# Table stage of a token-embedding, attention and mixture-of-experts kernel: 128 partitions in place of 125, the angle product on TensorE, rounding on ScalarE, clamps and scalings on GpSimd

## What is computed

```python
# token table: rows with is_num become sines of number times frequency
freqs = arange(1, 129)
scaled = num_value / 1000
sin_table = sin(scaled[:, None] * freqs[None, :])        # 12500 x 128
table = where(is_num[:, None], sin_table, weight)
h = table[x]                                             # x: 128 x 128 ids
# attention with mixed heads (8 heads of 64, 128 sequences of 128 tokens)
h = h + attn(layernorm(h), Wq, Wkv, scale, mix_pre, mix_post, Wout, bout)
# a shared expert and two banks of 8 experts, top 1, capacity 1280 rows
h = h + ffn(layernorm(h), ...)
```

## Time and profile before

| | us |
|---|---|
| median of three executions | 1666.71 |
| lowest and highest | 1663.58, 1667.42 |
| span of the profiled execution, first to last instruction | 1659.7 |
| the median above that span | 7.0 |
| busy in the span: PE, PEld, DVE, ACT, POOL | 1495.3, 1377.3, 1119.0, 1149.3, 1129.5 |
| first instruction of the stage after `setup` | 113.40 |

### The profile page before, as it was taken

One profiled execution on the slowest core, in us unless ns is written; L12 is line 12 of the kernel. 1 busy time (PEld: TensorE's weight loads), 2 busy tenths in 40 slices (PEclk: granted clock), 3 DMA queues, 4 the chain that ended last, 5 costly groups with the idle time before them and its releaser, 6 DMA issues. The chain is left out here.

```text
span 1659.7 us, 37390 instructions
## 1 busy us (share of the span) xinstructions
PE 1495.3 (90%) x11183; PEld 1377.3 (83%) x11183; DVE 1119.0 (67%) x2864; ACT 1149.3 (69%) x3478; POOL 1129.5 (68%) x1105
## 2 busy tenths in 40 slices
PE   4306999999999999999999999987999988879999
PEld 2105999999989989989989999877999988879999
DVE  8957778878878777877878887752332444456555
ACT  3416988888888888888888888853555544445554
POOL 8835556787878878878878786656700767766665
PEclk8659999999999999999999999998999999989999
DMA  3332220000000000000000000002443555533333
GB/s 132 133 111 94 105 90 15 28 27 27 18 19 19 17 18 16 14 15 14 15 15 15 14 15 7 3 5 62 110 114 106 135 137 141 130 77 87 86 87 84
DMA packets 112855, 97.75 MB, mean 59 GB/s; under 512 B 26417, under 2 KB 98285, under 8 KB 112676
## 3 DMA queue, kind: packets, MB, share of 16 engines
q1 hardware_dynamic: 90896, 58.18, 11.4%
q0 software_dynamic: 20480, 31.01, 8.3%
q10 hardware_dynamic: 1300, 6.40, 1.0%
HBM read 53.96 MB, written 52.54 MB: 64 GB/s over the span
## 5 line engine op out<-in xcount | busy, mean ns | idle before, releaser
L774 ACT ACTIVATE expd<-masked,nmax 128x128 f32<-128x128 f32 x1024 | 395.9, 393 | 0.0
L585 POOL TENSOR_TENSOR prob<-expd,rtotal 128x1024 f32<-128x1024 f32 x128 | 243.3, 1901 | 134.1 <-DVE rtotal L852 133.6
L869 DVE COPY_PREDICATED masked<-off_diag,ps_s 128x1024 f32<-128x1024 int32 x128 | 175.2, 1369 | 139.3 <-PE ps_s L672 139.3
L714 PE MATMUL ps_o<-u,probT 128*128 128x128 f32 x2048 | 249.1, 275 | 0.7 <-issue 0.7
L714 PEld LDWEIGHTS ps_o<-u,probT 128*128 128x128 f32 x2048 | 239.0, 191 | 0.9 <-issue 0.9
L1352 POOL DMA_INDIRECT fq_back<-answered_sp,fq_back_i x128 | 122.5, 957 | 137.2 <-DVE fq_back_i L1313 103.0
L774 ACT ACTIVATION_READ_ACCUMULATOR expd<-masked,nmax 128x1 f32 x1024 | 196.9, 192 | 0.0
L783 ACT ACTIVATE u<-ps_ut 128x1024 f32<-128x1024 f32 x128 | 131.4, 1027 | 68.8 <-PE ps_ut L725 68.8
L797 ACT ACTIVATE probT<-ps_ut 128x1024 f32<-128x1024 f32 x128 | 131.6, 1028 | 51.3 <-PE ps_ut L680 44.7
L884 DVE TENSOR_TENSOR w_lo<-ps_w,w_hi 128x512 fp32r<-128x512 f32 x256 | 163.9, 680 | 4.4 <-ACT w_hi L804 4.4
L804 ACT ACTIVATE w_hi<-ps_w 128x512 fp32r<-128x512 f32 x256 | 146.2, 596 | 16.5 <-PE ps_w L702 10.0
(11 more groups left out here) (236 smaller groups left out, 4099.0 us busy)
## 6 DMA issues: line engine op xcount, KB each, us to landing
out<-sh_res SPq DMA_DIRECT2D x56, 128.0 KB, 2.3
h_sb<-in_L_tok_weight SPq DMA_DIRECT2D x10, 625.0 KB
table<-h_sb ACTq DMA_DIRECT2D x10, 625.0 KB
sent_sp<-zeros SPq DMA_DIRECT2D x8, 640.0 KB, 3.0
sent_fq<-zeros SPq DMA_DIRECT2D x8, 640.0 KB, 2.9
rows<-sent_sp SPq DMA_DIRECT2D x40, 128.0 KB, 3.1
answered_sp<-sp_res SPq DMA_DIRECT2D x40, 128.0 KB
rows<-sent_fq SPq DMA_DIRECT2D x40, 128.0 KB, 3.6
```

The lines of the kernel that those rows point to most:

```text
L585: nc.gpsimd.tensor_tensor(prob[k % 2][:, :].rearrange("p (g j) -> p g j", g=H), expd[k % 2][:, :].rearrange("p (g j) -> p g j", g=H), rtot ...
L714: mm = nc.tensor.matmul(ps_o[:, 0:D], probT[k % 2][:, g * N:(g + 1) * N], u[k % 2][:, g * D:(g + 1) * D], start=(g == 0), stop=(g == H - 1))
L774: ins = nc.scalar.activation(expd[(k - 1) % 2][:, g * N:(g + 1) * N], masked[(k - 1) % 2][:, g * N:(g + 1) * N], ACT.Exp, bias=nmax[(k - 1 ...
L869: nc.vector.copy_predicated(masked[k % 2][:, :].rearrange("p (g j) -> p g j", g=H), off_diag[:, :].unsqueeze(1).to_broadcast([P, H, N]), p ...
```

## The change

- The table lies over 128 partitions, 97 rows in each, and the 84 rows that are left over form a 98th column on 84 partitions. Chunks have 8 rows (128 x 1024 values, 512 KB); there are 12 of these and one of 2 rows, 13 in all.
- PE turns the numbers (13 small products into `numT`), and then makes the angles: `numT` (8 numbers by 128 partitions) times `freq`, a block diagonal of 8 x 1024, into PSUM (`ps_a`, two buffers). Two products of 512 columns a chunk, with 8 rows of contraction.
- ACT finds the whole turns in two passes (1024 values from PSUM, then in place in SBUF), with the rounding constant as its bias, and takes the sine in place.
- DVE's two steps now read and write `ps_a`, the second writes `angle` in SBUF. DVE puts the sines of chunk c-2 where it was c-1.
- POOL clamps each chunk, and scales the 8 pieces with one instruction each (`mix`), and fills `masked`.
- `ps_m` holds both matrices in turn, so the fifth product waits for the low part of the first matrix.
- SP loads one chunk ahead of the other inputs, keeps four in flight, and issues all stores itself, after the loads.

The core of the diff:

```diff
-VP = 125
-VR = VOCAB // VP
-VC = 10
+VR = VOCAB // P
+REST = VOCAB - VR * P
+VS = VR + 1
+VC = 8
+CHUNKS = -(-VS // VC)
...
+        ps_a = [pb(f"ps_a{k}", CH) for k in range(2)]
+        ps_m = pb("ps_m", H * D)
+        ps_t = pb("ps_t", 512)
+        ps_c = pb("ps_c", 512)
...
+            def clamp(c):
+                a = angle[c % 3][:, 0:rows_of(c) * D]
+                pool.wait_ge(S["reduced"], c + 1)
+                nc.gpsimd.tensor_scalar(a, a, PI_BELOW, -PI_BELOW, ALU.min, ALU.max).then_inc(S["clamped"], 1)
+
+            def mix(c):
+                nc.gpsimd.tensor_tensor(mixed[:, c, :].rearrange("p (g d) -> p g d", g=H),
+                                        mix_src[:, c, :].unsqueeze(1).to_broadcast([P, H, D]),
+                                        mix_co[:, c, :].unsqueeze(2).to_broadcast([P, H, D]), ALU.mult).then_inc(S["mixed"], 1)
+
+            def prefill(k):
+                link.inc(nc.gpsimd.tensor_copy(masked[k][:, :].rearrange("p (g j) -> p g j", g=H),
+                                               diag[:, :].unsqueeze(2).to_broadcast([P, H, N])))
+
+            for c in range(CHUNKS):
+                clamp(c)
+                if c == 2:
+                    pool.wait_ge(S["coef_out"], 2)
+                    pool.wait_ge(S["wT_out"], 1)
+                if 2 <= c < 2 + 2 * HC:
+                    mix(c - 2)
+                if c == 2 + 2 * HC:
+                    prefill(0)
+                    prefill(1)
...
+            link(nc.gpsimd.memset(zeros[:, :], 0.0))
...
+            sp.dma_start(num_i[:, 0:VR], num_value[0:P * VR].rearrange("(p r) -> p r", p=P)).then_inc(S["num"], 16)
+            sp.dma_start(isn[:, 0:VR], is_num[0:P * VR].rearrange("(p r) -> p r", p=P)).then_inc(S["num"], 16)
+            sp.wait_ge(S["made"], made["pads"])
+            sp.dma_start(num_i[0:REST, VR:VS], num_value[P * VR:VOCAB].rearrange("(p o) -> p o", o=1)).then_inc(S["num"], 16)
+            sp.dma_start(rest_isn[0:REST, 0:1], is_num[P * VR:VOCAB].rearrange("(p o) -> p o", o=1)).then_inc(S["num"], 16)
+            sp.dma_start(h_sb[:, cols(0)], w_main[:, cols(0)]).then_inc(s_row[0], 16)
...
+            for c in range(1, CHUNKS - 1):
+                need(sp, s_row[c % 4], 16 * (c // 4))
+                sp.dma_start(h_sb[:, cols(c)], w_main[:, cols(c)]).then_inc(s_row[c % 4], 16)
+            one = slice((CHUNKS - 1) * CH, VR * D)
+            sp.wait_ge(s_row[(CHUNKS - 1) % 4], 16 * ((CHUNKS - 1) // 4))
+            sp.dma_start(h_sb[:, one], w_main[:, one]).then_inc(s_row[(CHUNKS - 1) % 4], 16)
+            sp.dma_start(h_sb[0:REST, LAST_COL], weight[P * VR:VOCAB, :]).then_inc(s_row[(CHUNKS - 1) % 4], 16)
...
+            for c in range(CHUNKS - 1):
+                sp.wait_ge(S["done"], c + 1)
+                sp.dma_start(t_main[:, cols(c)], h_sb[:, cols(c)]).then_inc(S["put"], 16)
+            sp.wait_ge(S["done"], CHUNKS)
+            sp.dma_start(t_main[:, one], h_sb[:, one]).then_inc(S["put"], 16)
+            sp.dma_start(table[P * VR:VOCAB, :], h_sb[0:REST, LAST_COL]).then_inc(S["put"], 16)
+            sp.wait_ge(S["put"], 16 * (5 + CHUNKS + 1))
...
+            def whole_turns(c):
+                w = rows_of(c) * D
+                act.wait_ge(S["angle"], c + 1)
+                need(act, S["reduced"], c - 1)
+                t = turns[c % 2][:, 0:w]
+                nc.scalar.activation(t, ps_a[c % 2][:, 0:w], ACT.Copy, bias=ROUND, scale=INV_TWO_PI).then_inc(S["whole"], 1)
+                act.wait_ge(S["whole"], 2 * c + 1)
+                nc.scalar.activation(t, t, ACT.Copy, bias=-ROUND).then_inc(S["whole"], 1)
+
+            def sines(c):
+                a = angle[c % 3][:, 0:rows_of(c) * D]
+                act.wait_ge(S["clamped"], c + 1)
+                nc.scalar.activation(a, a, ACT.Sin).then_inc(S["sine"], 1)
+
+            for c in range(CHUNKS + 1):
+                if c < CHUNKS:
+                    whole_turns(c)
                 if c:
+                    sines(c - 1)
+                if 1 <= c <= 3:
+                    act.wait_ge(S["wT"], c)
+                    dst = (mix_src[:, 0:HC, :], wkT[:, :, :], wvT[:, :, :])[c - 1]
+                    nc.scalar.activation(dst.rearrange("p c n -> p (c n)"), ps_t[:, :], ACT.Copy).then_inc(S["wT_out"], 1)
+                if c == 1:
+                    act.wait_ge(S["coefd"], 1)
+                    nc.scalar.activation(mix_co[:, :, :].rearrange("p c h -> p (c h)"), ps_c[:, 0:2 * HC * H], ACT.Copy).then_inc(S["coef_out"], 1)
+                    nc.scalar.activation(diag[:, :], ps_c[:, 128:128 + H], ACT.Copy).then_inc(S["coef_out"], 1)
+                for w in range(2):
+                    if c == (8, CHUNKS)[w]:
+                        act.wait_ge(S["M"], w + 1)
+                        nc.scalar.activation(mats["MN"[w] + "_hi"][:, :], ps_m[:, :], ACT.Copy).then_inc(S["hi"], 1)
...
+            def angles(c):
+                n = rows_of(c)
+                pe.wait_ge(S["made"], made["freq"])
+                pe.wait_ge(S["numT_out"], 1 if c < 2 else 4)
+                need(pe, S["reduced"], c - 1)
+                for at in range(0, n * D, 512):
+                    w = min(512, n * D - at)
+                    ins = nc.tensor.matmul(ps_a[c % 2][:, at:at + w], numT[0:n, c * P:(c + 1) * P], freq[0:n, at:at + w],
+                                           start=True, stop=True)
+                ins.then_inc(S["angle"], 1)
...
+            def product(c):
+                w = c // HC
+                if c == HC:
+                    pe.wait_ge(S["lo"], 1)
+                if c == 0:
+                    pe.wait_ge(S["wT_out"], 2)
+                if c == HC:
+                    pe.wait_ge(S["wT_out"], 3)
+                pe.wait_ge(S["mixed"], c + 1)
+                for half in range(2):
+                    at = slice(half * 512, (half + 1) * 512)
+                    ins = nc.tensor.matmul(ps_m[:, at], (wkT, wvT)[w][:, c % HC, :], mixed[:, c, at],
+                                           start=(c % HC == 0), stop=(c % HC == HC - 1))
+                if c % HC == HC - 1:
+                    ins.then_inc(S["M"], 1)
+
+            for c in range(CHUNKS):
+                angles(c)
+                if c == 1:
+                    turn(0)
+                    coefficients()
+                if c in (2, 3):
+                    turn(c - 1)
+                if 4 <= c < 4 + HC:
+                    product(c - 4)
+                if c >= 9:
+                    product(HC + c - 9)
...
+            def reduce(c):
+                w = rows_of(c) * D
+                a, t, out = ps_a[c % 2][:, 0:w], turns[c % 2][:, 0:w], angle[c % 3][:, 0:w]
+                dve.wait_ge(S["whole"], 2 * c + 2)
+                link(nc.vector.scalar_tensor_tensor(a, t, -TWO_PI_HI, a, ALU.mult, ALU.add))
+                nc.vector.scalar_tensor_tensor(out, t, -TWO_PI_LO, a, ALU.mult, ALU.add).then_inc(S["reduced"], 1)
 
             def put_sines(c):
+                n = rows_of(c)
+                dve.wait_ge(s_row[c % 4], 16 * (c // 4 + 1 + (c == CHUNKS - 1)))
+                dve.wait_ge(S["sine"], c + 1)
+                nc.vector.copy_predicated(h_sb[:, cols(c)].rearrange("p (r d) -> p r d", r=n),
+                                          mask[:, c * VC:c * VC + n].unsqueeze(2).to_broadcast([P, n, D]),
+                                          angle[c % 3][:, 0:n * D].rearrange("p (r d) -> p r d", r=n)).then_inc(S["done"], 1)
...
+                reduce(c)
+                if c >= 2:
+                    put_sines(c - 2)
+                if c == 2:
+                    dve.wait_ge(S["coefd"], 1)
                     link.inc(nc.vector.tensor_copy(ids[:, :], ps_c[:, 256:384]))
+                    dve.wait_ge(S["made"], made["rank_i"])
+                    link.inc(nc.vector.tensor_copy(C.rank[:, :], C.rank_i[:, :]))
+                if c == 9:
+                    low(0)
+            put_sines(CHUNKS - 2)
             put_sines(CHUNKS - 1)
+            low(1)
```

More of the change, by code:

```diff
@@ L266, in setup @@
-        block = s.enter_context(nc.Block())
-        def chunk(c):
-            return slice(c * CH, (c + 1) * CH)
+        ps_a = [pb(f"ps_a{k}", CH) for k in range(2)]
+        ps_m = pb("ps_m", H * D)
+        ps_t = pb("ps_t", 512)
+        ps_c = pb("ps_c", 512)
+        names = ("made", "num", "num_f", "numT", "numT_out", "angle", "whole", "reduced", "clamped", "sine", "done", "put",
+                 "weights", "wT", "wT_out", "coef", "coefd", "coef_out", "mixed", "M", "hi", "lo")
+        S = {n: sem("s_" + n) for n in names}
@@ L375, in _ @@
         @block.tensor
         def _(pe):
-            pe.wait_ge(s_const, 8)
-            pe.wait_ge(s_small, 112)
-            for c in range(HC):
-                nc.tensor.transpose(ps_t[0][:, c * P:(c + 1) * P], wq[:, c * P:(c + 1) * P], ident[:, :])
-                nc.tensor.transpose(ps_t[1][:, c * P:(c + 1) * P], wkv[:, c * P:(c + 1) * P], ident[:, :])
```

(26 more changed lines are left out.)

242 lines of the change are left out of this document (100 added, 142 removed).

## The result

| us | before | changed |
|---|---|---|
| median (lowest to highest) | 1666.99 (1663.58 to 1667.42) | 1642.39 (1639.63 to 1644.99) |
| profiled execution, its own time | 1661.5 | 1641.4 |
| its span | 1659.7 | 1639.6 |
| barrier (SP's first issue of the next stage) | 113.40 | 90.94 |
| barrier to the first masked copy of attention | 25.7 | 28.8 |

The changed kernel takes 0.9862 of the time before [0.9844, 0.9879] (brackets behind a ratio hold its 95% interval), 24.6 us less. An execution's own time stands 1.8 us above its span (1641.4 to 1639.6); 1661.5 is worked out with that. The barrier is the end of the stage, read as SP's first issue behind it.

A forecast was written before the change was run, and what follows sets the result against it. DVE's list and 132 GB/s transfers bound the stage together. Front 29.9, chunks to 60.7, wait to 75.2 and tail put the barrier at 89.7, 23.7 us earlier: span 1636.0 plus 7.0 gives 1643.0, range 1635 to 1658.

The forecast's parts named there:

- Two limits side by side: Stage before: DVE's list to 104.4 and transfers to 112.4; lifting only one leaves the other holding.
- Transfers: Large loads and stores: 128 partitions give 410 GB/s instead of 132, 12.8 MB in 31 us, under DVE's work.
- DVE's new steps: DVE's two steps per chunk: 1.22 us each, not lengthened by POOL because one operand lies in PSUM.
- The slower rival: POOL lengthens DVE's new steps as the old: 6.9 per chunk, 30 us in all, total 1673; 4 in 100.
- Period 4.3: Middle chunks 3 to 8: 8.6 us for two chunks, 4.3 each, six chunks ending at 55.7.
- a ring: Middle chunks: clamp, sine, ACT's passes, DVE's reducing and a 1.28 wait for the copy in sequence, 7.9 for two chunks.
- The front, 29.9 for chunk 2: Stage start: numbers ready at 7.5, first chunk reduced at 19.4, chunk 2 reduced at 29.9 us.
- From chunk 4 on I take it so: PE in the middle chunks: 3.4 us of full-clock work in 4.3 keeps the clock up from chunk 4.
- The rival of the low clock: PE stays at 1.2 GHz since 8-row products don't hold it; 6.9 us a chunk, total 1657; 12 in 100.
- The hole: After chunk 9: fifth product waits for `M_lo`, chunk 10's angles queue behind; 14.5 us, from 60.7 to 75.2.
- The tail: Chunks 11 and 12, last copies, store issues and landing: from 75.2 to the barrier at 89.7.
- From the barrier to the total: After the stage: the barrier's 23.7 us gain passes whole to the span, plus 7.0 from span to median: 1643.0.

The follow-up runs named there:

- 1: The kernel before with each large transfer cut into partitions 0 to 111 and 112 to 124; 1658.10, ratio 0.9964.
- 2: The changed kernel with its large transfers cut into 125 and 3 partitions; 1658.25, ratio 0.9970.
- rows128_step: The changed kernel with angle products padded to 128 rows and DVE's second step reading two SBUF inputs; one execution, barrier at 93.66, no total given.
- 7: The changed kernel with one wait added, so POOL builds the frequencies only after DVE has made the numbers; ratio 0.9879.
- after_again: The changed kernel unedited, run again on another chip; 1790.12, ratio 0.9896 to before on that chip, barrier at 96.13.
- 8: The changed kernel with 50 unused products of 512 columns on PE ahead of its attention list; ratio 0.9868.

## Why the prediction was right, and where not

The time came out within 1 us, 1643.0 and 1642.4, and the mechanism was the one forecast: two limits side by side, both lifted, and a new wait after `M_lo`. That it came so near is luck: the steps behind it were off by up to 3.7 us each, and their errors cancel.

- **Two limits side by side.** Right, and the experiments 1 and 2 show it: 6.2, 3.8, and 22.5 together.
- **Transfers.** Right: the share of 0.31 is gone with the 125 partitions, and came back with them in 2. The Trainium skill, "DMA: Bandwidth & Descriptors", section "Why a DMA increments its semaphore by 16 and not by 1", says that the engines are the largest k up to 16 that divides the slowest dimension of both sides, here the partitions. The rows agree: a share of 0.94 with 112, 0.33 with 125.
- **DVE's new steps**, 1.22 each: right throughout. The slower rival (steps as long as before) needed what rows128_step made, 2.45.
- **Period 4.3**: without low clock it was 3.85. I had added 0.7 of handovers per two chunks and 1.28 for the clamp behind the copy. The clamp does wait, 0.96 (2.00 for 1.04). The Trainium skill, "SBUF — State Buffer", section "Who interferes with whom", states the lock, and the trace agrees on it (2.00 and, in rows128_step, 2.45). But in the changed kernel it costs next to nothing, because 2.00 + 1.89 on POOL are no more than 0.1 above DVE's 3.83. I had priced a ring where two engines' own lists bind.
- **The front, 29.9 for chunk 2**: 32.6. The number steps took 4.65 us (4.53 to 9.18) beside POOL's building of `freq`, and 2.5 without it (7). I had let POOL's work there cost nothing. The 13 pieces took 5.3, not 2.8, since each is two records at 0.21 and I took one. But the first angles were through 2.0 us after their start (14.65 to 16.67), not 3.8: the clock that I had down was up. So the first reduced chunk came at 21.3 for 19.4, and the third angles began at 24.2 for 23.4. The other 2.1 of the 2.7 come behind that: these angles took 3.78, where I had the clock up and 1.7. I had the clock the wrong way round twice.
- **"From chunk 4 on I take it so"**, the clock at full: the step that failed most. Chunks 3 to 8 took 29.5 where 25.8 stood; with 128 rows, 24.8. The rival of the low clock was given 12 in 100; it held for about half the stage (18 to 41 and 52 to 55 us, and the product after the hole), and where it held a chunk with angles and piece takes PE 7.42, not the 6.9 of the prediction. Its argument (few rows don't hold it) was right as far as the runs with 8 and with 128 rows go, and my argument against it (short gaps) was not: PE had no gaps at all from 18 to 40 us. The Trainium skill, "TensorE: Matmul & The Clock Gate", Part 1, says that the clock follows how busy PE has been, and that sustained matmul work releases it; the rows of 18 to 40 us do not agree, and they decide.
- **The hole**, 14.5: 12.8 (66.0 to 78.8). Half right by luck of the clock: the first product took 3.78 for the 3.4 of the sum, the angles behind it 2.06 instead of 3.8. In after_again both took 3.78.
- **The tail**: from chunk 10 to the barrier 12.1, predicted 14.5. Chunks 11 and 12 were 0.7 shorter together, the last copies 0.5, and from the last copy's end to the barrier there were 3.2 for 4.3.
- **The barrier**: 90.94 for 89.7. The errors nearly cancel: front +2.7, chunks 3 to 8 +3.7, chunk 9 -1.1 (3.9 for 5.0), hole -1.7, tail -2.4, together +1.2.
- **From the barrier to the total.** I took 23.7 for both. The barrier moved 22.5, and the first masked copy of attention comes 28.8 behind it, not 25.7, so the span is only 20.1 shorter. PE runs at 0.50 until 120 there; 8 shows that the clock is what moves this copy, and after_again, with 26.2, that the changed kernel needn't lose there. No rival had that. The 7.0 us between span and median were not overhead, which is 1.8; the profiled execution of before was 5.2 below its median, that of the changed kernel 1.0 below. So the medians lie 24.6 apart where the two spans lie 20.1 apart. That the right total came out of this is luck too.

## What to carry to other kernels

Where two limits lie side by side, cost both, and expect little from an edit that moves one. Ask of a long series of matmuls how many rows it contracts, not only how busy PE is: here padding 8 rows to 128 with zeros took 4.7 us off chunks 3 to 8 (one profile of each kernel; the clock in all twelve says the same), and cost nothing once DVE filled the pads while it waited. And take one profile of a stage in which the clock changes as one draw, not as the kernel's time: compare an edit with several profiles of the kernel without it.
